# Which engine makes the low part of x: the subtraction of the attention steps put on GpSimd in place of VectorE

## The reference

```python
xn = layernorm(x)
x  = x + attention(xn) + experts(xn)
# attention: gated linear attention, 4 heads, chunks of 64 tokens
q, k, v, g = xn @ Wq, xn @ Wk, xn @ Wv, xn @ Wg
gk = log_sigmoid(xn @ Wgk + bgk) / 16          # decay per token and head
o  = decayed, causal attention of q, k, v       # inside a chunk and through a state
on = o * rsqrt(mean(o * o) + 1e-5) * gnorm_w
attention = (on * g * sigmoid(g)) @ Wo
# experts: each token goes to the one expert of 8 with the highest router logit
experts = expert_w * (gelu(xn @ w1[e] + b1[e]) @ w2[e] + b2[e])
```

## Time and profile before

| | |
|---|---|
| median of 3 runs | 391.74 us |
| the runs | 391.74, 391.71, 392.69 us |
| profiled execution: its own time | 392.97 us |
| profiled execution: span from the first to the last instruction | 391.2 us |
| mean granted TensorE clock, share of full speed | 0.985 |
| TensorE busy | 373.5 us (95%) |
| VectorE busy | 312.9 us (80%) |
| ScalarE busy | 291.9 us (75%) |
| GpSimd busy | 278.1 us (71%) |

### The profile page before, as it was taken

The page is one execution under the profiler, slowest core; times in us unless marked ns, Lnnn a source line. Parts: engine busy times, 40 slices in busy tenths (PEclk is TensorE's granted clock), DMA queues, the critical chain, the costliest instruction groups (busy, mean ns, idle before and its releaser), DMA issues.

```text
span 391.2 us, 13871 instructions
## 1 busy us (share of the span) xinstructions
PE 373.5 (95%) x3947; PEld 321.4 (82%) x3947; DVE 312.9 (80%) x859; ACT 291.9 (75%) x889; POOL 278.1 (71%) x245
## 2 busy tenths in 40 slices
PE   7997899999999999999999999999999999999991
PEld 7666677778787878787878777899999999999991
DVE  5987799988888888888888879677777687787761
ACT  4887886888888888888878886566666666666670
POOL 8002353788778888888788883178888888888887
PEclk9996999999999999999999999999999999999997
DMA  8935579555655535575655333146555555555540
GB/s 232 253 137 160 183 226 335 152 172 182 169 179 177 164 107 159 171 189 164 191 164 170 105 103 85 41 67 75 67 72 69 64 72 72 70 75 70 71 41 6
DMA packets 59107, 51.45 MB, mean 132 GB/s; under 512 B 7201, under 2 KB 51393, under 8 KB 59073
## 3 DMA queue, kind: packets, MB, share of 16 engines
q1 hardware_dynamic: 45936, 42.07, 37.5%
q0 software_dynamic: 12272, 8.54, 15.8%
q10 hardware_dynamic: 864, 0.40, 0.4%
HBM read 33.14 MB, written 18.30 MB: 131 GB/s over the span
## 4 chain that ended last, share of the span: by engine, by line
PE 85%; DVE 4%; DMA 3%; ACT 3%; issue 2%; SPq 2%; POOL 1%; DVEq 0%; ACTq 0%; POOLq 0%
PE psVG L965 16%; PE psA L977 16%; PE psVG L771 12%; PE psT L859 8%; PE psO L825 7%; PE psQK L757 5%; PE psT L851 4%; PE psVG L790 4%; PE psO L839 4%; PE psKS L814 3%; ACT E L1148 2%; SPq L355 2%; DMA x_all<-in_L_attn_x_dram 1%; POOL out_dram L619 1%; DMA gcB<-decay_rows 1%
## 5 line engine op out<-in xcount | busy, mean ns | idle before, releaser
L619 POOL DMA_INDIRECT out_dram<-yw,sidx x71 | 112.6, 1586 | 28.8 <-DVE yw L1687 11.2
L1148 ACT ACTIVATE E<-gcB,ngc 128x128 f32<-128x128 f32 x256 | 78.4, 394 | 0.4 <-DMA gcB<-decay_rows 0.4
L577 POOL DMA_INDIRECT sorted_rows<-x_all,pos_i x64 | 65.3, 1020 | 13.4 <-issue 13.1
L561 POOL TENSOR_TENSOR rms<-msn,neg_half 128x8 f32<-128x8 f32 x32 | 53.5, 1673 | 24.7 <-DVE msn L1475 16.5
L554 POOL TENSOR_SCALAR_AFFINE_SELECT E<-E 128x1024 f32<-128x1024 f32 x32 | 35.1, 1096 | 42.8 <-ACT E L1148 30.4
L1130 ACT ACTIVATE th<-psVG,x_all 128x256 f32<-128x256 f32 x64 | 26.8, 470 | 21.6 <-issue 11.9
L825 PE MATMUL psO<-v_sb,pr 128*64 128x64 f32 x1024 | 36.3, 225 | 2.7 <-DVE pr L1504 2.7
L977 PE MATMUL psA<-xT_all,v_sb 128*128 x288 | 38.1, 275 | 0.4 <-DVE yb L1685 0.4
L965 PE MATMUL psVG<-xgT,gcB 128*128 128x128 f32 x288 | 38.0, 275 | 0.0
L825 PEld LDWEIGHTS psO<-v_sb,pr 128*64 128x64 f32 x1024 | 34.8, 141 | 3.4 <-issue 3.2
L977 PE MATMUL psA<-xT_all,th 128*128 x280 | 37.5, 277 | 0.1
(11 more groups left out here) (209 smaller groups left out, 943.1 us busy)
## 6 DMA issues: line engine op xcount, KB each, us to landing
gcB<-decay_rows SPq DMA_DIRECT2D x32, 512.0 KB
sorted_rows<-blank SPq DMA_DIRECT2D x12, 396.0 KB, 5.7
xg<-sorted_rows SPq DMA_DIRECT2D x71, 66.0 KB
x_all<-in_L_attn_x_dram SPq DMA_DIRECT2D x16, 256.0 KB, 5.3
out_dram<-res SPq DMA_DIRECT2D x32, 128.0 KB
eqB<-decay_exp_rows SPq DMA_DIRECT2D x32, 64.0 KB
w1b<-in_L_ffn_w_dram SPq DMA_DIRECT2D x8, 256.0 KB
xT_all<-in_L_ffn_w_dram SPq DMA_DIRECT2D x32, 64.0 KB
```

The source lines that it names most:

```text
L561: nc.gpsimd.tensor_tensor(rms[:], msn[:], neg_half[:, 0:2 * H], ALU.pow).then_inc(rms_ready, 1)
L577: nc.gpsimd.indirect_dma_start(out=sorted_dram, out_offset=bass.IndirectOffsetOnAxis(ap=pos_i[:, t:t + 1], axis=0), in_=x_all[:, t, :], in ...
L619: nc.gpsimd.indirect_dma_start(out=out_rows, out_offset=bass.IndirectOffsetOnAxis(ap=sidx[j][:], axis=0), in_=yw[j][:], in_offset=None, bo ...
L1148: last = nc.scalar.activation(E[j][:, k, h * P:(h + 1) * P], gcB[j][:, k * H + h, :], ACT.Exp, bias=ngcf[:, bass.ds((s * 2 + k) * H + h, 1)])
```

## The change

In steps 2 to 29 VectorE no longer makes x_lo of sequence s+2. GpSimd makes it in its own step s, with the same operation on the same operands, ahead of rms_step(s-1). The splits of sequences 0 to 3 stay on VectorE; for that of sequence 4 GpSimd waits until these four are counted.

```diff
+            def split_lo(i, j):
+                s = i * 2 + j
+                if s == 4:
+                    pool.wait_ge(lo_ready, 4)
+                pool.wait_ge(hi_ready, s + 1)
+                nc.gpsimd.tensor_tensor(x_lo[j][:], xT_all[:, s, :], x_hi[j][:].bitcast(F32), ALU.subtract).then_inc(lo_ready, 1)
...
                 if s >= 1:
                     if s >= 2:
                         pool.wait_ge(dve_on, s - 1)
+                    if 2 <= s < SEQS - 2:
+                        split_lo(*divmod(s + 2, 2))
                     rms_step(*divmod(s - 1, 2))
...
                 if inside(i, j, 0, SEQS):
                     make_gate(i, j)
-                if inside(i, j, 2, SEQS):
-                    split_lo(*turn(i, j, 2, 2))
                 if inside(i, j, -1, SEQS):
                     mean_square(*turn(i, j, -1, 2))
```

## The result

The kernel after took 396.78 us (median of 4, 395.37 to 398.15), the kernel before 392.22 (median of 4): ratio 1.0129, 95% interval 1.0103 to 1.0155. The change costs 4.6 us by these medians and 5.0 by the ratio (one of the four runs of the kernel before, 397.26 us, lies far above the other three, 391.71 to 392.69); the forecast was 392.5 with 395.2 as its upper end. The profiled execution of the kernel after took 396.48 with a span of 394.8.

What follows compares the result with a forecast made beforehand. TensorE's chain was taken as the bound, with 1.20 us a pair free on GpSimd; 1.15 us held at c 0.65 less 0.4 gained in steps 2 and 6 gave +0.75 on 391.74, so 392.5, range 390.8 to 395.2.

Steps and rivals of the forecast that it cites:

- Step 2: First changed step: ms could start 0.7 us earlier without x_lo, of which 0.3 was counted as gain.
- The cost of the late first rows: After step 29: placed completes up to 1 us later, covered by 3.56 us before the first read, costed at nothing.
- Rival B: Odd steps: VectorE answers sooner after msn, worth 1.5 us, a time of 389.8; chance 0.10.
- The price c: Time of one added 128x256 subtraction on GpSimd: taken as 0.65 us, bounds 0.578 and 0.766.
- rival A: GpSimd becomes the bound in earnest, subtraction 0.68 us or more: net +1.5 to +3.5 us; chance 0.28.
- held time: Time TensorE is held by GpSimd's lateness over steps 6 to 29: 24 c - 14.45, 1.15 us at 0.65.
- The gap between the subtraction and rms: On GpSimd in each step: taken as zero; each 0.05 us of it would cost 1.2 us.
- Rival C: Even steps: the subtraction starts ahead of msn and holds it, 0.21 us a step, net +2.1 (393.8); chance 0.07.
- The mask's wait of 0.49 for on: GpSimd in the odd step: 0.49 us of waiting before the mask, taken out as free time.
- the floor: GpSimd's own work without waits: 6.55 us an even step, 5.24 an odd one, 11.79 of 12.99 a pair.
- the gap from the last placing to the next operation: On GpSimd, between a step's last placing DMA and rms: 0.11 us, counted in each step's own time.
- 0.69 us of slack: Odd step: how much later rms could end before delaying VectorE's product on; with another 0.09, together 0.78.

Runs made afterwards that it cites:

- relief alone: Kernel after, but GpSimd subtracts only 1 of x_lo's 256 columns, the other 255 stale: 390.58 us against 392.45 for the kernel before, ratio 0.994.
- the three kernels without the pause in which GpSimd carries the whole load: Kernel after with subtraction between placings; second adjacent placing replaced by a 1200-column memset; subtraction cut to one column plus a 540-column memset: ratios 1.0436, 1.0323, 1.0376.
- The run meant to isolate it: Kernel after, GpSimd subtracting one column of 256, then a memset of 540 columns: 400.87 us against 386.49 for the kernel before, ratio 1.0376.

## Why the prediction was wrong

*Right.* The bound was read where it is: VectorE's relief is worth next to nothing in the regular steps (relief alone: pair 12.93 against 12.99), and GpSimd's free time is what the edit spends. Step 2 gained 7.79 - 7.35 = 0.44 us where I counted 0.3, its msn held by the subtraction as I said (45.86, 0.42 us). The cost of the late first rows was nothing: issued at 239.01, first read at 242.70. The subtraction lay within its bounds of 0.578 to 0.766. Rival B did not happen.

*Wrong, step by step.* Timeline of the kernel after, GpSimd, rms of steps 6 and 29:

```profile
74.91 1.67 POOL L561 TENSOR_TENSOR rms<-msn,neg_half 128x8 f32<-128x8 f32 x1
...
230.86 1.68 POOL L561 TENSOR_TENSOR rms<-msn,neg_half 128x8 f32<-128x8 f32 x1
```

From the one to the other the kernel after took 155.95 us. My sum, without the first c, gives 136.24 + 23 c, which is 151.19 at 0.65. The 4.76 us of difference:

- The price c: 0.737 in place of 0.65, 23 x 0.087 = 2.0 us. This alone would have made the change slower (my rival A, held time 24 x 0.737 - 14.45 = 3.2, net +2.8). I leaned "nearer to the lower end"; the line through both rows gave 0.766, and it was the better guide.
- The gap between the subtraction and rms, taken as zero: 0.12 in nearly every step, about 2.5 us. This is the term that failed in kind. Rival C had the mechanism but put it in even steps only, and ruled it out because "msn goes first" once GpSimd is late. The rows show the opposite: the subtraction is the first operation that a late GpSimd starts, before msn is there, in both parities.
- The mask's wait of 0.49 for on, taken out of the floor whole: 0.19 of it stayed in 11 odd steps, 2.1 us. On is late in the odd step because the squares are (1.39 us after the gate) or because msn is held until 149.57: from msn to the end of on (152.55) VectorE works without a gap, both stand in that one chain, and no run separates the two.
- In the other direction, the gap from the last placing to the next operation is 0.03 and not 0.11: 23 x 0.08 = 1.84 us less.

2.0 + 2.5 + 2.1 - 1.84 = 4.8. The two errors of the floor nearly cancel, which is luck; the hold and the price remain.

The path was wrong too. The sum let GpSimd's lateness reach TensorE through rms and the product on, after 0.69 us of slack, and a sign of being right was rms ending 0.15 us before on. In the kernel after, on starts 0.4 to 0.7 us behind the end of rms in every step from 8 to 28 (step 17: 151.33 and 151.86), so rms releases it in none. What the rows leave is the held msn, with the products pr right behind it, and the second placing with the pause behind it; their shares are not separated. Only in the three kernels without the pause in which GpSimd carries the whole load (pairs of 13.78 to 13.97) does on follow rms, by 0.09 us (160.03 and 160.12).

*How far this is shown.* That the load alone costs the loss is shown by the two runs that add load and no relief (1.6% and 1.2%), with the reserve that VectorE's x_lo is held by the mask in both. That the hold is a hold is shown by msn beside the memset, 0.17 us; its price, 0.12 a step, is read from the rows and from the difference of 0.17 a pair between those two runs, in which x_lo differs too. The run meant to isolate it fell in a job without the pause and shows another balance, so the price has no run of its own. The kernel after was not timed in a job without the pause; that it would lose more there (3.2 to 4.4%, as its three near relatives did) is an inference from them.

*What stays open.* What the pause is. It is tied in time to the end of the second placing (it ends 0.71 to 0.75 us after it in the rows above) and moves with it, it stops SyncE as well as TensorE, and it was absent from all kernels of two jobs, one of them on a chip on which another job had it. Why, no run shows. Nothing tried beat both kernels but the relief alone, which leaves work out.

## What to carry to other kernels

Before moving work to an engine that is not on the chain, add up that engine's own round without its waits, and count each small operation of the other engine that the moved one will hold, and each release it will delay: here 0.12 us of hold a step cost more than the error in the price. When the receiving engine becomes the bound, the order of starts around it changes, and other holds appear (a DMA issue of 1.03 us became 1.50). An experiment that takes the suspected cause away must be judged against a baseline of the same job, and its trace read for what took the cause's place.

## What the runs showed of the hardware

- A GpSimd subtraction of 128x256 is 0.737 us, one of 128x1 0.204, a memset of 768 columns 0.75, of 540 columns 0.565, of 8 columns 0.12.
- A VectorE operation with two inputs in SBUF is held to the end of a GpSimd operation that reads SBUF and is under way, however small the VectorE operation is: msn of 8 columns went from 0.17 to 0.47 and 0.55 us beside the subtraction and to 1.15 beside the mask, x_lo from 0.42 to 1.45 beside the mask. Beside a memset msn kept its 0.17.
- It works the other way round too: in four kernels, with the pause and without, an indirect DMA that GpSimd issued 0.07 to 0.14 us after VectorE's product on (two inputs in SBUF) had started took 1.46 to 1.53 us in place of 1.03. It ended 0.90 to 0.92 us after the end of on each time, 79 times.
- The mask held x_lo and msn even where these start up to 0.07 and 0.22 us before it by the records.
- Two indirect DMAs in a row from GpSimd were followed by a pause of TensorE and SyncE until 0.7 us after the second, in some jobs and not in others. The kernel before took 390.7 to 392.5 us in the jobs with it and 386.3 to 386.5 in the two without.
